# Moving batch 0's routing in among the weight parts of a routed FFN kernel

## The reference

```python
att  = softmax(x, -1) / sqrt(1024)                   # per batch, 1024 x 1024
adj  = side * cond * att;  diagonal = -inf
mask = 1.0 where adj is among the 10240 largest of its batch, else 0.0
scores = softmax(mask @ G);  value, indices = top_k(scores, 2)   # 2 experts a token
w = one_hot(indices) weighted by value
gated = silu(mask @ gate_w.T) * (mask @ up_w.T)      # for each expert
out = (gated * w) @ down_w.T + ((mask @ lora_A.T) * w) @ lora_B.T
return x + out
```

## Time and profile before

| what | value |
|---|---|
| median of 3 runs | 802.29 us (801.61 to 802.94) |
| the profiled execution's own time | 801.54 us |
| its span, first to last instruction | 799.8 us |
| mean granted TensorE clock | 0.840 |
| TensorE busy | 500.9 us (63%) |
| VectorE busy | 523.6 us (65%) |
| ScalarE busy | 442.2 us (55%) |
| GpSimd busy | 389.5 us (49%) |

### The profile page before, as it was taken

How to read it: one execution, slowest core, us unless ns; L and a number is a source line. 1 busy time by engine, 2 the same in 40 slices (tenths; PEclk the granted TensorE clock), 3 DMA queues, 4 the chain that set the end, 5 groups by cost and what they waited for, 6 DMA issues and landing times.

```text
span 799.8 us, 13618 instructions
## 1 busy us (share of the span) xinstructions
PE 500.9 (63%) x3682; PEld 330.4 (41%) x3682; DVE 523.6 (65%) x1242; ACT 442.2 (55%) x655; POOL 389.5 (49%) x337
## 2 busy tenths in 40 slices
PE   0211187259878882788777717977669469788800
PEld 0200076146545551455445414544436246455400
DVE  5768789857598686776786867757872723343245
ACT  6687278738845476297445653973336345455300
POOL 7114200045366123588886136768971177877400
PEclk9755599669999895799999957998988869999865
DMA  9990060013312453368368733575478238767469
GB/s 317 360 269 0 3 261 28 0 49 113 113 74 91 166 217 107 125 226 283 133 220 272 299 102 131 206 261 175 169 252 326 94 102 287 262 207 260 164 259 381
DMA packets 76984, 147.29 MB, mean 184 GB/s; under 512 B 21475, under 2 KB 30699, under 8 KB 76400
## 3 DMA queue, kind: packets, MB, share of 16 engines
q1 hardware_dynamic: 59248, 104.40, 38.4%
q0 software_dynamic: 17664, 41.98, 14.7%
HBM read 95.47 MB, written 69.21 MB: 206 GB/s over the span
## 4 chain that ended last, share of the span: by engine, by line
DVE 20%; DMA 18%; issue 15%; POOL 14%; PE 13%; ACT 8%; DVEq 7%; SPq 2%; POOLq 1%; ACTq 0%
DMA put_rows<-y,where 5%; DMA piece<-put_rows 5%; DMA out_dram<-piece 5%; PE pa L690 4%; DVE mask L1075 4%; ACT mask L805 3%; POOL piece L538 3%; POOL xg L521 3%; DVE small L1037 3%; POOL piece L541 3%; DMA w<-put_rows 2%; ACT y L862 2%; DVEq L1364 2%; DVEq L1031 1%; DVE g_parts L1365 1%
## 5 line engine op out<-in xcount | busy, mean ns | idle before, releaser
L690 PE MATMUL pa<-w,xt 128*128 x1472 | 209.2, 296 | 5.4 <-issue 4.3
L862 ACT ACTIVATE y<-pc,where 128x512 f32<-128x512 f32 x184 | 121.7, 688 | 150.8 <-DMA put_rows<-y,where 94.6
L690 PEld LDWEIGHTS pa<-w,xt 128*128 128x128 f16 x1472 | 149.2, 102 | 74.1 <-issue 25.7
L529 POOL DMA_INDIRECT put_rows<-y,where x92 | 92.1, 1001 | 134.4 <-ACT y L862 114.0
L521 POOL DMA_INDIRECT xg<-mask_rows,where x92 | 99.1, 1078 | 115.8 <-DVEq L1349 95.0
L1357 DVE SCALAR_TENSOR_TENSOR g_full<-pa,where,s_act 128x144 f32<-128x144 f32 x92 | 33.5, 364 | 177.2 <-ACT s_act L854 177.2
L849 ACT ACTIVATE xt<-pb 128x1024 f16<-128x1024 uint8 x92 | 94.2, 1024 | 46.7 <-PE pb L677 46.5
L713 PE MATMUL pc<-wd,gt 128*128 x184 | 75.6, 411 | 13.1 <-ACT y L862 11.9
L714 PE MATMUL pc<-wd,gt 128*128 x184 | 75.9, 413 | 0.0
L715 PE MATMUL pc<-wd,gt 128*128 x184 | 75.5, 410 | 0.0
L716 PE MATMUL pc<-lb,gt 128*128 x184 | 75.5, 410 | 0.0
(11 more groups left out here) (208 smaller groups left out, 864.9 us busy)
## 6 DMA issues: line engine op xcount, KB each, us to landing
piece<-put_rows SPq DMA_DIRECT2D x96, 256.0 KB, 3.9
v<-in_x_dram SPq DMA_DIRECT2D x40, 512.0 KB, 8.5
piece<-in_x_dram SPq DMA_DIRECT2D x48, 256.0 KB, 2.9
out_dram<-piece SPq DMA_DIRECT2D x48, 256.0 KB
w<-put_rows SPq DMA_DIRECT2D x16, 512.0 KB, 9.6
w<-in_L_ffn_gate_w_dram SPq DMA_DIRECT2D x8, 512.0 KB, 10.3
w<-in_L_ffn_up_w_dram SPq DMA_DIRECT2D x8, 512.0 KB, 8.3
wd<-in_L_ffn_down_w_dram SPq DMA_DIRECT2D x8, 512.0 KB, 9.5
```

Source lines behind the costliest of these rows:

```text
L529: pool.indirect_dma_start(out=put_rows[n % 2], out_offset=bass.IndirectOffsetOnAxis(ap=put_row[n][:, i:i + 1], axis=0), in_=y[:, g % NY, : ...
L690: last = pe.matmul(l1[g % 2], xt[:, g % 2, t, :], w1[:, bass.ds(e, 1), t, k, :].rearrange("p o n -> p (o n)"), start=(t == 0 and k == 0), ...
L862: nc.scalar.activation(y[:, g % NY, half * HALF:(half + 1) * HALF], pc[:, half, :], ACT.Copy, scale=y_scale[n][:, i:i + 1]).then_inc(y_rea ...
```

## The change

Batch 0's mask store is issued ahead of the next batch's loads. TensorE turns and scores the mask's eight chunks with only expert 1's turn in between; expert 2's turn, `rank` and `place_slots` follow, then experts 3 to 7 and the LoRA factors. ScalarE copies four chunks, cuts expert 1, copies four chunks, cuts expert 2, takes the probabilities, then cuts experts 3 to 7 with one exponential of batch 1 behind each, the LoRA cuts, the four LoRA stores and the last three exponentials. VectorE cuts experts 0 and 1, runs the five functions of the route with the eight maxima between them, cuts expert 2 ahead of `take_slots`, then cuts experts 3 to 7 and the LoRA remainder. Routes of batches 1 to 3 stay as they are.

```diff
             def move_mask(n):
                 sp.wait_ge(mask_ready, n + 1)
+                if n == 0:
+                    store_mask(n)
                 if n + 1 < B:
                     load_side(n + 1)
                     load_x(n + 1)
...
-                sp.dma_start(mask_rows[n % 2].rearrange("(p c) h -> p (c h)", c=C),
-                             mask_8).then_inc(mask_stored, 16)
+                if n > 0:
+                    store_mask(n)
@@ tensor
                 score(0, c)
-                if c + 1 < E:
-                    turn_expert(c + 1)
-            turn_lora()
+                if c == C // 2 - 2:
+                    turn_expert(1)
+            turn_expert(2)
             rank(0)
             place_slots(0)
+            for e in range(3, E):
+                turn_expert(e)
+            turn_lora()
@@ scalar
-            store_mt(0, 0)
-            for c in range(1, C):
-                store_mt(0, c)
-                cut_high(c)
-            cut_lora_high()
...
-            store_lora(0)
+            for c in range(C):
+                store_mt(0, c)
+                if c == C // 2 - 1:
+                    cut_high(1)
+            cut_high(2)
             probabilities(0)
-            for k in range(1, E // 2):
+            for e in range(3, E):
+                cut_high(e)
+                exponential(1, e - 3)
+            cut_lora_high()
+            for k in range(E // 2):
                 store_lora(k)
-            for c in range(C):
+            for c in range(E - 3, C):
                 exponential(1, c)
@@ vector
-            for e in range(E):
+            cut_low(0)
+            cut_low(1)
+            choose(0)
+            for c in range(3):
+                maximum(1, c)
+            weigh(0)
+            for c in range(3, 5):
+                maximum(1, c)
+            place_pairs(0)
+            for c in range(5, C):
+                maximum(1, c)
+            fill_table(0)
+            cut_low(2)
+            take_slots(0)
+            for e in range(3, E):
                 cut_low(e)
-                maximum(1, e)
             cut_lora_low()
-            route(0)
```

More of the change, by code:

```diff
@@ L384, in store_piece, with store_mask @@
                              piece[:, u % NC, 0, :]).then_inc(piece_stored[u % NC], 16)
+            def store_mask(n):
+                sp.dma_start(mask_rows[n % 2].rearrange("(p c) h -> p (c h)", c=C),
+                             mask_8).then_inc(mask_stored, 16)
             def move_mask(n):
                 sp.wait_ge(mask_ready, n + 1)
+                if n == 0:
+                    store_mask(n)
                 if n + 1 < B:
```

## The result

The changed kernel takes 819.66 us (median of 4 runs, 816.18 to 820.62), the kernel before in the same comparison 801.95 (800.98 to 802.94): a ratio of 1.022, 95% interval 1.0193 to 1.0247. Forecast were 821.9 and slower. The profiled execution has a span of 817.5, 17.7 more than before.

The account below looks back on a forecast made before the run. VectorE's program order was taken to set the stage, with rounds of 4.94 through the PSUM banks. Profiled 801.54 plus 19.6 at the first tile gave 821.1, or 821.9 in median terms; 8-in-10 range 816 to 827.

Parts of the forecast that it names:

- Mask scored first: ScalarE's eight mask copies with expert 1's turn between: scores ready at 117.3, when VectorE begins choosing.
- Rival 5: Scores come no earlier because copies and turns collide; routing and rounds both later, above 827 us; chance 0.04.
- Routing: VectorE from 117.3: route, eight maxima and expert 2's cuts take 30.8; routed at 148.1, 11.1 earlier.
- Experts 3 to 7: Expert 3's first low cut at 148.7, rounds still 4.94 through the PSUM bank loop, expert 7's cut at 168.5.
- rival 2: VectorE bounds the rounds: without a maximum each takes 3.6, 5.4 less in four rounds, 816.5 us; chance 0.08.
- The tail: ScalarE's high cuts, exponentials, LoRA cuts and stores from expert 7 on: first tile copy at 183.9, 19.6 later.
- Mask stored first: Batch 0's store lands by 113.7 at worst, before choosing; x loads start 0.45 later; both cost nothing.
- The clock: TensorE: expert 3's turn starts at the lower level, taking 3.17; no row shows the clock of the later rounds.
- rival 1: Experts 3 to 7's rounds run at TensorE's lower clock: 4.4 more, 826.3 us; chance 0.12.
- Carrying it through: After the first tile the program is the old one, so the whole 19.6 delay reaches the end.
- rival 3: Batch 0's tile loop gives back 5 through idle time and earlier exponentials: 817 us; chance 0.08.
- Rival 4: First tile released by its gather, copy at 153.2, 791 us, if the fourth LoRA store ends before 152; chance 0.02.

Follow-up runs that it names:

- the first experiment: The kernel before, with only batch 0's mask store issued ahead of the next x's loads: 802.59 us, ratio 0.9991 to 1.0032.

## Why the prediction was right

- *Mask scored first:* choosing at 117.74 (117.3 said). Expert 1's two matrices took 3.67 instead of 3.17, at a granted clock of 0.50 (104 to 108; before, 100 to 104, it was 0.62); that is the half microsecond. Rival 5 (scores no earlier) falls.
- *Routing:* routed at 147.1, 148.1 said. From choosing on it took 29.4 instead of 30.8, of which 1.0 shows, as choosing began 0.4 later. Maxima in a row cost 1.13 each, start to start, not 1.21, which is half of the difference; placing was 0.4 shorter, as an idle of 0.44 in it is gone. That nothing needed runs beside the maxima is true of five: the first three cover the probabilities.
- *Experts 3 to 7:* first cut 148.12 (148.7; the prediction's own terms, with four handovers of 0.1, make 148.9), rounds 4.94 as said. Expert 3's first two matrices took 3.24 (3.17 said) at a granted clock of 0.59 (143 to 147), the lower level for most of it, as said. Removing the maximum shortened none of them: rival 2 falls.
- *The tail:* 15.40 from expert 7's cut to the copy, as worked out (183.9 - 168.5). The experiments took 7.0 and 3.0 out of it singly, 7.7 together.
- *Mask stored first:* nothing, as said. The x loads were issued 1.15 later (99.56 instead of 98.41), not 0.45, which no maximum was early enough to feel. Landing times of the changed kernel's four stores, answering to the earlier trace rows:

```profile
DMA to landing us min/median/max: 4.2/14.5/15.6
```

  The shortest was 12.8 before, and it was batch 0's; the 4.2 is again batch 0's own (the same view from 90 to 130 alone has only this store), far inside the bound. The order of the loads matters only where a maximum comes early (the first experiment).
- *The clock:* 1.00 from 150 to 170 with TensorE busy 13.88 of 20. So rival 1 falls, and the clock swings that the Trainium skill describes for groups that cycle through PSUM banks with short idles between them (TensorE: Matmul & The Clock Gate, A second HAM failure mode: psum-queue depth-cycling) are not seen in these rounds. The lower bound's first tiles at full clock didn't come either: 0.50 from 184 to 190, as before from 163 to 168.
- *Carrying it through:* 18.94 at the first tile, 17.7 at the end. The forecast has 19.6 for both. The 0.7 comes from the routing above; the 1.2 that the loops gave back is the term that was a little off, far from the 5 of rival 3. Both lie in the scatter that one kernel shows (1.4 at the first tile; the loops lasted 630.3 to 639.0). So the stage was worked out right, while the end within 2.2 of the forecast is in part luck.
- *Rival 4* falls by its own point: the fourth LoRA store ended at 180.0, not before 152.

## What to carry to other kernels

Work that stands beside a latency loop is free only there; moved to a place where its engine is the one everybody waits for, it costs its full duration, and the loop it left doesn't get shorter. Before a result is moved forward, ask which other program the consumer is behind: an early route is worth nothing while the weights come late. If a serial block has to come early, spread it over the loop's rounds instead of putting it in one piece, so that the loop goes on behind it; what this can gain is the latency at the block's end (here the gather), for the block still costs its engine's time.

## What the runs showed of the hardware

- The 1 MB mask store of batch 0 landed in 4.2 to 4.6 in the seven profiled executions that issue it ahead of 4 MB of loads, and in 12.8 and 13.7 in the two that issue it behind them. In the kernel with this part alone the first x chunk came 2.2 later, 0.8 of it because the loads were issued later (99.23 instead of 98.41).
- Two executions of one kernel had different granted clocks in the same stretches (0.70 and 0.84 from 104 to 112, 0.59 and 0.85 from 143 to 147), and expert 3's cut, for which only short turns on TensorE are needed, moved by 1.4 with it.
